# The last gather of two of a step's rows, fetched pixel by pixel from SyncE's and ScalarE's queues

## What is computed

```python
x = x + _L0_conv_ref(_gn(x), ...)   # 3x3 convolution
x = x + _L1_conv_ref(_gn(x), ...)   # deformable convolution, below
x = x + _L2_conv_ref(_gn(x), ...)   # focal modulation: depthwise 3x3, 5x5, 7x7 with gelu, gates
x = x + _L3_conv_ref(_gn(x), ...)   # layer norms, two gated products, a product over rows, a gate
```

```python
idx = (yi * W + xi).reshape(B, -1, 1)
v = jnp.take_along_axis(flat, idx, axis=1)
out = wa * gather(y0i, x0i) + wb * gather(y1i, x0i) + wc * gather(y0i, x1i) + wd * gather(y1i, x1i)
```

## Time and profile before

| | |
|---|---|
| median of 3 runs | 12372.07 us (12347.44 to 12374.3) |
| span of the profiled execution | 17350.5 us |
| gathers issued by GpSimd | 9216 |
| steps | 128 |
| granted TensorE clock, mean | 0.694 |
| HBM read, written | 1069 MB, 245 MB |

### The profile page before, as it was taken

One profiled execution on the slowest core, in us unless ns is written; L12 is line 12 of the kernel. 1 busy time (PEld: TensorE's weight loads), 2 busy tenths in 40 slices (PEclk: granted clock), 3 DMA queues, 4 the chain that ended last, 5 costly groups with the idle time before them and its releaser, 6 DMA issues.

```text
span 17350.5 us, 102336 instructions
## 1 busy us (share of the span) xinstructions
PE 8037.3 (46%) x30934; PEld 5581.5 (32%) x30934; DVE 5165.4 (30%) x5993; ACT 1769.5 (10%) x2822; POOL 8759.5 (50%) x9300
## 2 busy tenths in 40 slices
PE   4444444445345544443335555344325555443358
PEld 2223223223234432232224443232223443222245
DVE  2222222322333233233222233223223223222323
ACT  1001101110000011100000001110000001110014
POOL 4555555455554555455554455555555444545530
PEclk7667677667667776666667777666667777666679
DMA  2222222222223321222123321222112332122233
GB/s 78 68 60 66 78 62 70 72 61 77 61 75 98 98 60 48 63 80 59 43 61 99 98 84 45 57 77 68 46 52 77 98 98 61 48 64 77 60 124 118
DMA packets 878203, 1254.74 MB, mean 72 GB/s; under 512 B 183384, under 2 KB 663064, under 8 KB 859992
## 3 DMA queue, kind: packets, MB, share of 16 engines
q0 software_dynamic: 294912, 604.57, 13.7%
q1 hardware_dynamic: 511784, 596.71, 10.7%
q10 hardware_dynamic: 71344, 51.39, 0.9%
HBM read 1069.42 MB, written 245.43 MB: 76 GB/s over the span
## 4 chain that ended last, share of the span: by engine, by line
another core or an unknown queue 40%; PE 20%; issue 19%; DVE 10%; ACT 3%; PEldq 2%; PEld 1%; SPq 1%; DMA 1%; ACTq 1%; DVEq 1%
PE acc L1307 8%; PE stage L1163 6%; DVE srow L1685 5%; PE stage L1035 2%; PEldq L483 2%; DVE gathered L1678 2%; PE pt L1294 1%; ACT stt L1008 1%; PEld acc L1307 1%; PE stage L1102 1%; PE stage L1081 1%; DMA off<-offs 1%; DVE wtn L1647 0%; SPq L694 0%
## 5 line engine op out<-in xcount | busy, mean ns | idle before, releaser
L543 POOL DMA_INDIRECT gathered<-table,idx x9216 | 8708.9, 945 | 7844.0 <-issue 4412.7
L1307 PE MATMUL acc<-stt,room 128*128 128x256 f32 (+2 forms) x15360 | 4368.5, 438 | 4763.0 <-ACT stt L1008 2491.7
L1307 PEld LDWEIGHTS acc<-stt,room 128*128 128x128 f32 (+1 forms) x15360 | 3242.4, 221 | 5803.8 <-issue 2728.6
L1685 DVE TENSOR_REDUCE srow<-gathered 128x576 f32<-128x2304 f32 x512 | 2097.1, 4096 | 324.7 <-remote 207.2
L1163 PE MATMUL stage<-room 128*128 128x128 f32 x6784 | 1035.3, 303 | 1067.5 <-issue 1049.5
L1163 PEld LDWEIGHTS stage<-room 128*128 128x128 f32 x6784 | 962.5, 218 | 1139.8 <-issue 1134.0
L1678 DVE TENSOR_TENSOR gathered<-gathered,wtb 128x2304 f32<-128x2304 f32 x512 | 1304.4, 2548 | 1.2 <-issue 1.2
L1008 ACT ACTIVATE stt<-pt 128x1024 f32<-128x1024 f32 (+1 forms) x512 | 415.6, 812 | 8375.5 <-remote 4988.2
L1666 DVE SCALAR_TENSOR_TENSOR xs<-acc,fused,xr 128x256 f32<-128x256 f32 x128 | 61.7, 482 | 3747.9 <-PE acc L1307 2206.0
L1035 PE MATMUL stage<-room,mat 128*128 128x512 f32 (+1 forms) x1360 | 776.2, 694 | 841.1 <-issue 338.9
L1294 PE MATMUL pt<-mat,srow 128*128 128x128 f32 x2048 | 427.2, 337 | 1475.6 <-DVE srow L1685 1250.7
(11 more groups left out here) (212 smaller groups left out, 4575.2 us busy)
## 6 DMA issues: line engine op xcount, KB each, us to landing
gathered<-table,idx POOLq DMA_INDIRECT x9216
room<-toep SPq DMA_DIRECT2D x48, 1792.0 KB, 7.0
room<-toep SPq DMA_DIRECT2D x64, 1280.0 KB, 8.0
room<-toep SPq DMA_DIRECT2D x64, 768.0 KB
table<-room SPq DMA_DIRECT2D x64, 512.0 KB
toep<-in_taps SPq DMA_DIRECT2D x128, 224.0 KB
gathered<-toep SPq DMA_DIRECT2D x16, 1792.0 KB, 7.0
toep<-in_taps SPq DMA_DIRECT2D x128, 160.0 KB
```

The lines of the kernel that those rows point to most:

```text
L543: nc.gpsimd.indirect_dma_start(gat[r][:, k % K9 * G + k // K9, :], None, table[b].rearrange("(n e) -> n e", e=PAIR), bass.IndirectOffsetOn ...
L1307: ins = nc.tensor.matmul(sums_of[:, pairs, :], wk[0:kk, m, dx, at:at + P], stt[0:kk, slots, m, dx:dx + W], start=start and m == 0 and dx == 0,
L1685: nc.vector.tensor_reduce(srow[r % 2][:].rearrange("p (s c) -> p s c", c=CG), gat[r][:].rearrange("p s (q c) -> p s c q", q=4), AX.X, ALU. ...
```

## The change

Of two of a step's four rows, 3 and 0, the last of the 18 gathers is taken from GpSimd. For row 3 SyncE, for row 0 ScalarE fetches the same 128 entries with 128 DMAs of 512 bytes each.

- VectorE writes these 128 byte addresses (entry x 256 plus the group's offset) as integers into `pixel_at[r]` (two tensor_scalar of 128x1 a step), right after the indices.
- The engine turns the column into a row with one DMA (`pixel_row[r]`), waits for it and for the buffer's last sum, and then works in eight chunks: it reads 16 addresses into registers and issues 16 DMAs, one row of `gathered` each, from the table at that byte address.
- SyncE's chunks (`fetch`) stand at phases 0.5, 1, ... 4 of the same step. They are merged with SyncE's other instructions of the step; it waits for the sum of row 3 of the step before.
- ScalarE's chunks stand at 3r + 3 and 3r + 4, two after each row's copies, and serve row 0 of the next step; the first step's are fetched at the start, before the second tile of offsets.
- VectorE waits for 17 gathers and for the 128 pixels of such a row.
- To free semaphores, the four `lg_s` of the roots become one with a running count; that alters no order.

The diff, without the lines that only rename `lg_s`:

```diff
@@ -23,6 +23,7 @@
 U32 = mybir.dt.uint32
+U8 = mybir.dt.uint8
 ALU = mybir.AluOpType
...
@@ -46,6 +47,9 @@
 STEPS = NB * PER
+FETCHED = {3: GK - 1, 0: GK - 1}
+BY_SP, BY_ACT = 3, 0
+CHUNK = 16
 ENTRY = 4 * CG
...
@@ -120,6 +124,16 @@
         k = min((t, k) for k, t in enumerate(times) if t is not None)[1]
+        times[k] = next(flows[k], None)
+def merged(*flows):
+    times = [next(f, None) for f in flows]
+    while any(t is not None for t in times):
+        t, k = min((t, k) for k, t in enumerate(times) if t is not None)
+        yield t
         times[k] = next(flows[k], None)
...
@@ -255,6 +269,8 @@
         idx = sb("idx", [P, ROWS, GK], U32)
+        pixel_at = {r: sb(f"pixel_at{r}", [P, 1], I32) for r in FETCHED}
+        pixel_row = {r: sb(f"pixel_row{r}", [1, P], I32) for r in FETCHED}
         wtn = sb("wtn", [P, ROWS, GK, 4])
...
@@ -434,6 +450,13 @@
         turned_full, full_ready = sems("turned_full", "full_ready")
+        act_given, act_row_in = sems("act_given", "act_row_in")
+        pixels_given = {BY_SP: composed, BY_ACT: act_given}
+        pixel_row_in = {BY_SP: x_in[1], BY_ACT: act_row_in}
+        pixels_in = {BY_SP: x_in[2], BY_ACT: loaded}
+        GIVEN0 = {BY_SP: 2, BY_ACT: 0}
+        ROW0 = {BY_SP: 16, BY_ACT: 16}
+        PIXELS0 = {BY_SP: 16, BY_ACT: 16 * N_LOAD}
         (padded_c,) = sems("padded_c")
...
@@ -495,6 +518,21 @@
             return d[b].rearrange("c (h r) w -> r c h w", r=2)[par, :, ds(4 * t, 4), :]
+        def gathered_by_pool(r):
+            return GK - 1 if r in FETCHED else GK
+        def fetch_pixels(eng, engine, b, r, first):
+            k = FETCHED[r]
+            slot = k % K9 * G + k // K9
+            _, starts = nc.values_load_multi_w_load_instructions(
+                pixel_row[r][:, first:first + CHUNK], engines=[engine], min_val=0, max_val=4 * PAIR * (G * TABLE - 1),
+                skip_runtime_bounds_check_because="the coordinates are clipped to the image")
+            for p, start in enumerate(starts, first):
+                eng.dma_start(gat[r][p:p + 1, slot, :].bitcast(U8), table[b].bitcast(U8)[ds(start, 4 * ENTRY)].unsqueeze(0))\
+                    .then_inc(pixels_in[r], 16)
...
@@ -539,7 +577,7 @@
                         pool.sem_inc(started, 1)
-                        for k in range(GK):
+                        for k in range(gathered_by_pool(r)):
                             nc.gpsimd.indirect_dma_start(
...
@@ -760,7 +798,24 @@
+                def fetch(n, b, at):
+                    r = BY_SP
+                    yield at
+                    sp.wait_ge(pixels_given[r], GIVEN0[r] + n + 1)
+                    sp.dma_start(pixel_row[r][:], pixel_at[r][:]).then_inc(pixel_row_in[r], 16)
+                    sp.wait_ge(pixel_row_in[r], ROW0[r] + 16 * n + 16)
+                    sp.sem_inc(started, 1)
+                    sp.wait_ge(summed, ROWS * n + r + 1)
+                    sp.sem_inc(started, 1)
+                    for first in range(0, P, CHUNK):
+                        yield at + 4 * first / P
+                        fetch_pixels(sp, mybir.EngineType.SP, b, r, first)
                 def step(n, b, i):
+                    return merged(step_body(n, b, i), fetch(n, b, 0.5))
+                def step_body(n, b, i):
                     yield 0
...
@@ -998,8 +1053,31 @@
+                def give_row(n):
+                    act.wait_ge(pixels_given[BY_ACT], GIVEN0[BY_ACT] + n + 1)
+                    act.dma_start(pixel_row[BY_ACT][:], pixel_at[BY_ACT][:]).then_inc(pixel_row_in[BY_ACT], 16)
+                def row_given(n):
+                    act.wait_ge(pixel_row_in[BY_ACT], ROW0[BY_ACT] + 16 * n + 16)
+                    act.sem_inc(started, 1)
+                    act.wait_ge(summed, ROWS * n + BY_ACT + 1)
+                    act.sem_inc(started, 1)
+                def start():
+                    give_row(0)
+                    row_given(0)
+                    for first in range(0, P, CHUNK):
+                        fetch_pixels(act, mybir.EngineType.Activation, 0, BY_ACT, first)
                 def step(n, b, i):
+                    last = isinstance(n, int) and n == STEPS - 1
+                    nb = b + 1 if isinstance(i, int) and i == PER - 1 else b
+                    if not last:
+                        yield 1
+                        give_row(n + 1)
                     for r in range(ROWS):
...
@@ -1011,12 +1089,20 @@
                             .then_inc(st_ready, 1)
+                        if last:
+                            continue
+                        if r == 0:
+                            row_given(n + 1)
+                        for q in range(2 * r, 2 * r + 2):
+                            yield 3 * r + (3 if q % 2 == 0 else 4)
+                            fetch_pixels(act, mybir.EngineType.Activation, nb, BY_ACT, q * CHUNK)
...
                 act.sem_inc(right_entries, 2)
-                drive(act, meet, step, lambda: None, {"modulate": ln_and_exp, "close": ln_and_exp},
+                act.sem_inc(pixel_row_in[BY_ACT], 16)
+                drive(act, meet, step, start, {"modulate": ln_and_exp, "close": ln_and_exp},
                       {"conv_norm": norm, "shift": shift, "conv_shift": lower_part, "table_norm": norm,
...
@@ -1649,6 +1735,10 @@
                     then(tt(idxn[:], entry, gbase[:], ALU.add))
+                    for r, k in FETCHED.items():
+                        dve.wait_ge(pixel_row_in[r], ROW0[r] + 16 * n)
+                        ts(pixel_at[r][:], entry[:, r, k:k + 1], 4.0 * PAIR, 4.0 * PAIR * TABLE * (k // K9),
+                           ALU.mult, ALU.add).then_inc(pixels_given[r], 1)
                     then(ts(xy(base, 1), xy(base, 1), float(ROWS), None, ALU.add))
...
@@ -1669,7 +1759,9 @@
                     yield 3 * r
-                    dve.wait_ge(landed[r], 16 * GK * (n + 1))
+                    dve.wait_ge(landed[r], 16 * gathered_by_pool(r) * (n + 1))
+                    if r in FETCHED:
+                        dve.wait_ge(pixels_in[r], PIXELS0[r] + 16 * P * (n + 1))
                     if give:
...
```

More of the change, by code:

```diff
@@ L447, in build @@
                                              "sums", "dw_chain", "mixed"))
-        q_p, q_s, m_p, xo_s, m_cen_p, m_sq_s, m_var_p, m_lg_s, m_rs_s, m_y_s, m_o_p, m_added = sems(
-            "q_p", "q_s", "m_p", "xo_s", "m_cen_p", "m_sq_s", "m_var_p", "m_lg_s", "m_rs_s", "m_y_s",
+        q_p, q_s, m_p, xo_s, m_cen_p, m_sq_s, m_var_p, m_rs_s, m_y_s, m_o_p, m_added = sems(
+            "q_p", "q_s", "m_p", "xo_s", "m_cen_p", "m_sq_s", "m_var_p", "m_rs_s", "m_y_s",
             "m_o_p", "m_added")
         ca_in = sems(*(f"ca_in{u}" for u in range(4)))
-        t_cen_p, t_sq_s, t_var_p, t_lg_s, t_rs_s, t_y_s, ab_p, g_p, ab_s, g_s = sems(
-            "t_cen_p", "t_sq_s", "t_var_p", "t_lg_s", "t_rs_s", "t_y_s", "ab_p", "g_p", "ab_s", "g_s")
+        t_cen_p, t_sq_s, t_var_p, t_rs_s, t_y_s, ab_p, g_p, ab_s, g_s = sems(
+            "t_cen_p", "t_sq_s", "t_var_p", "t_rs_s", "t_y_s", "ab_p", "g_p", "ab_s", "g_s")
         abg_out = sems(*(f"abg_out{u}" for u in range(4)))
@@ L459, in build @@
         ab_in, s_out = (sems(*(f"{n}{u}" for u in range(4))) for n in ("ab_in", "s_out"))
-        c_cen_p, c_sq_s, c_var_p, c_lg_s, c_rs_s, c_y_s, c_o_p, lin_s, res_s = sems(
-            "c_cen_p", "c_sq_s", "c_var_p", "c_lg_s", "c_rs_s", "c_y_s", "c_o_p", "lin_s", "res_s")
+        c_cen_p, c_sq_s, c_var_p, c_rs_s, c_y_s, c_o_p, lin_s, res_s, lg_s = sems(
+            "c_cen_p", "c_sq_s", "c_var_p", "c_rs_s", "c_y_s", "c_o_p", "lin_s", "res_s", "lg_s")
         s_in, g_in, res_out = (sems(*(f"{n}{u}" for u in range(4))) for n in ("s_in", "g_in", "res_out"))
@@ L904, in depthwise, with roots @@
                         act.dma_start(group(mixd, b, 2 * i + u), mix[u]).then_inc(mix_out[u], 16)
-                def roots(n, count, eps_, var_p, lg_s, y_s, rs_s):
+                def roots(n, count, eps_, var_p, y_s, rs_s, before):
                     for u in range(count + 1):
@@ L912, in roots @@
                         if u:
-                            act.wait_ge(lg_s, n(u - 1) + 1)
+                            act.wait_ge(lg_s, n(u - 1) + before + 1)
                             act.wait_ge(y_s, n(u - 1) + 1)
@@ L933, in modulate @@
                     yield 5
-                    roots(n, flight(b), eps[:, 1:2], m_var_p, m_lg_s, m_y_s, m_rs_s)
+                    roots(n, flight(b), eps[:, 1:2], m_var_p, m_y_s, m_rs_s, 2 * b * TB)
                 def operands(b, i):
@@ L944, in operands @@
                     ln_and_exp(b)
-                    roots(n, flight(b), eps[:, 0:1], t_var_p, t_lg_s, t_y_s, t_rs_s)
+                    roots(n, flight(b), eps[:, 0:1], t_var_p, t_y_s, t_rs_s, (2 * b + 1) * TB)
                     yield 7
@@ L989, in close @@
                     yield 5
-                    roots(n, flight(b), eps[:, 0:1], c_var_p, c_lg_s, c_y_s, c_rs_s)
```

(1 more changed line is left out.)

## The result

The changed kernel takes 13453.6 us (median of 4 runs, 13447.5 to 13459.9), the kernel before, on the same chip, 12373.2. The ratio is 1.087, with a 95% interval of 1.086 to 1.089: 1080 us slower, and 650 above the upper end of the range.

A forecast was written before the change was run, and what follows sets the result against it. GpSimd's gather pitch was taken to bound the kernel before, and SyncE's fetch chain the changed depthwise steps: 12372 - 320 (gathers saved) + 390 (depthwise loss) = 12442, say 12440 us, range 12040 to 12800.

The forecast's parts named there:

- The bound and the gathers' saving: GpSimd's gather pitch of 1.248 us bounds every step; two gathers fewer in each of 128 steps save 320 us.
- The gaps come from being recorded: Profiled execution: some 5000 us of gaps between gathers come from an engine slowed by recording; unrecorded, GpSimd hardly waits.
- The price of the fetch: On SyncE and ScalarE: a step's 128 pixel DMAs and address reads occupy the engine for 54 us, bounds 45 to 92.
- hidden: Rival: the depthwise chain stays short enough that GpSimd remains the bound, 12052 to 12100 us; chance 0.27.
- SyncE's block in the depthwise stage: In all 24 depthwise steps the second bands queue behind SyncE's whole fetch; three images lose 390 us.
- T to T: Depthwise step from one end of row 3's sum (T) to the next: 110 us, 23 more than GpSimd's 87.4.
- 20 + 54 = 74 is under 87.4: ScalarE's 20 us of work a step plus 54 of fetch stays below GpSimd's 87.4 us for 70 gathers.
- In other stages I take nothing: Outside the depthwise stage SyncE's late loads leave room; close comes near 95 us in 4 steps, absorbed; loss nothing.
- 54 us are absorbed per image: Depthwise stage: GpSimd's lead of three rows absorbs 54 us of the chain's excess once per image.
- The start, "nothing, at worst 10 us once": Kernel start: ScalarE fetches 128 pixels before the second offsets tile; costs nothing, at worst 10 us once.
- The two queues: Rival: SyncE's and ScalarE's issues hinder each other, 0.13 us more for each that overlaps; 12850 us, chance 0.05.
- The full sequencer: Rival: register reads cost 0.29 us each, a fetch 83 us on its engine; some 14300 us, chance 0.09.

The follow-up runs named there:

- e3: The kernel before with 17 gathers in rows 3 and 0 and nothing fetched in their place: 12047.7 us, ratio 0.974.
- e4: The kernel before, unchanged, profiled once more: 12372.9 us, with a profiled span of 12371.1 us.
- e1: The changed kernel without ScalarE's fetch (only SyncE fetches, row 0 keeps 18 gathers): 12634.2 us, ratio 1.021.
- e5: e1 with SyncE's eight chunks in bands, three of them ahead of the depthwise stage's second bands: 12218.3 us, ratio 0.989.
- e2: The changed kernel without SyncE's fetch (only ScalarE fetches, row 3 keeps 18 gathers): 12435.9 us, ratio 1.005.
- e12: e2 without ScalarE's last two chunks of eight, so 32 of 128 pixels aren't fetched: 12216.6 us, ratio 0.987.
- e13: e2 without ScalarE's first two chunks of eight, so 32 of 128 pixels aren't fetched: 12220.6 us, ratio 0.988.
- e10: e2 with ScalarE's eight chunks in two runs of four, behind the copies of rows 0 and 1: 13717.0 us, ratio 1.110.
- e7: The changed kernel with SyncE's chunks in bands as in e5, ScalarE's chunks as they were: 13131.4 us, ratio 1.063.
- e14: e7 without ScalarE's last two chunks (32 pixels not fetched): 12227.5 us, ratio 0.988.
- e15: e7 without ScalarE's first two chunks (32 pixels not fetched): 12787.3 us, ratio 1.034.

## Why the prediction was wrong, point by point

**The bound and the gathers' saving: right.** e3 gives 323.6 us for the 320 of the earlier trace rows.

**The gaps come from being recorded: wrong.** e4 recorded has none. The sum from 12372 was still right to make, since the gaps do not belong to the usual run.

**The price of the fetch: right.** 54 us was taken, bounds 45 to 92. A block took 50.8 us from its first pixel's issue, and with the first read of 1.2 us it is 52. A pixel was 0.33 us with 0.36 taken, as its issue was 0.223 to 0.228 and not the 0.28 drawn from the earlier trace rows. A chunk's read was 1.2 us with 1 taken. What decided for "hidden" was 38 us, so that rival fell for SyncE's one block.

**SyncE's block in the depthwise stage: right in mechanism, and in size in part by luck.** 112.2 us from T to T were measured with 110 predicted. The block began at T + 14.1 and not T + 8.5, as the pixel row took 7.9 us from its issue (4044.41) to what waited for it (4052.32), with 2.3 taken for the landing; the block was 2 us shorter, and from its end to TensorE's first pass it was 6.3 us, with 8.4 taken. The 390 us were for 70 gathers a step; for e1's 71 (88.8 us) the same sum gives 3 x (8 x 21.2 - 54) = 347 us, and 424 were measured (e1 against its floor): the first depthwise step of each image took 126 to 129 us and the others 112 to 116. e5, which moves nothing but those chunks, gives all but 8 to 29 us of it back.

**ScalarE, "20 + 54 = 74 is under 87.4": the step that failed.** Occupancy was compared where the chain counted. The earlier trace rows gave the 20 us of work, but not that each chunk stands between two turns with VectorE, on which row 0's pixels, the roots and gelus and so the sums depend. ScalarE's fetch cost 226 us alone (e2), by a threshold between 39 and 52 us (e12, e13), and up to 1507 with the same pixels in two runs of four (e10 against 12210). A row of before could have told it: in the earlier trace rows VectorE's sum at 5741.28 follows on an activation of ScalarE at 5738.53, with ScalarE itself waiting 4.15 us for TensorE. ScalarE is idle there because it waits as a link of the chain, not because it has time to spare.

**"In other stages I take nothing": the larger miss.** The steps of the changed kernel less those of e3 give 1366 us, and its first sum comes 42 later: together 1408, where the runs have 1406. The depthwise steps are 24 x (116.9 - 90.1) = 643 of it. The others were put at nothing: close 12 x (106.2 - 87.9) = 220, operands 12 x (99.3 - 87.8) = 138, triangle 6 x (109.5 - 86.9) = 136, the first stages' tables 12 x (96.3 - 87.7) = 103, modulate 12 x (92.3 - 85.2) = 85, all other stages 190, while the steps between the images are 152 shorter than in e3. The first close steps, 139 to 141 us, are 155 of the close stage's 220, and the first depthwise steps, 142 to 152, are 152 of the 643: the change of stage, where a late engine holds all, was not in the sum either. For SyncE alone the claim held: e1 and e5 average 85.8 and 87.8 us in the close stage. ScalarE's pairs were what was missed, and through the sigmoids, their store and the offsets table they also delayed SyncE's own start.

**"54 us are absorbed per image": right for one fetch, too much for two.** GpSimd's lead can be read from the timelines, as the time from the start of row 3's last gather to the end of that row's sum. In the fifth depthwise step of e1:

```profile
3957.77 0.94 POOL L581 DMA_INDIRECT gathered<-table,idx  x1 [0.30 <-issue]
...
4044.50 4.10 DVE L1779 TENSOR_REDUCE srow<-gathered 128x576 f32<-128x2304 f32 x1
```

That is 90.8 us. In e1 it is 11 us in the step ahead of each depthwise stage, 48 to 51 in its first step, and from the third to the last 91 to 94; in the operands stage it is back at 10 to 12. The stage's 24 steps are 623 us longer than 71 gathers, 424 us were lost, so some 66 us an image were absorbed, with 54 predicted. In the changed kernel it is 44, 23 and 21 us ahead of the stage in the three images, 82 to 99 in it, mostly 91, and then 48 to 110 through modulate, operands, triangle and close; only the last steps of an image, behind the close stage, three of them of 61 to 84 us, bring it back to 10. So it does come back once an image, as the prediction had it, but not between the stages, and what the later stages hold up is lost with little left to absorb it: beyond its pitch GpSimd waits some 520 us in the depthwise steps, 244 in close, 183 in modulate, 111 in triangle, 88 in operands and some 200 in the first image's stages, of 1445.

**The start, "nothing, at worst 10 us once": too low.** The first row 3's sum ended at 319.4 us, in e3 at 277.1, some 42 us later. GpSimd's first wait for it came only behind gather 210, so it went out of the lead at first; how much of it stayed to the end is not known.

**The rivals.** The two queues don't hinder each other: the issue medians are 223 and 228 ns with both engines fetching as with one. The Trainium skill (Perfetto Trace Analysis, DMA Instruction, HWDGE) says that the descriptor generator is shared and locked; no row here shows a wait for it. The full sequencer fell with the read's 0.075 us an address (1.2 / 16). The Trainium skill (DMA: Bandwidth & Descriptors, Issuing engines are not separate DMA queues) holds that more issuing engines save only the issue time, usually small. Here 256 gathers fewer to issue are worth 323.6 us of the whole (e3), and with 128 of them replaced from SyncE's queue 133 us are left (e5: 12351.4 - 12218.3).

Why in e7 the first pair's removal is worth so much less over the whole run than the last's, when in the close stage they are nearly equal, the lead shows in part. The steps in the table differ mostly in the depthwise stage (6.1 us less against 1.7) and the operands (10.4 against 7.4). In e14 the depthwise steps of 93 us fit into the lead, which grows from 30 to 57 us in the first image's stage, and GpSimd waits 29 us in all three, as in e3 (31). In e15 the steps of 97 find the lead used up by the third step (74 to 78 us from there on), and it waits 181. What stays open is how much of e14's 180 us above e3 is SyncE's chain and how much the three pairs left. A kernel in which both rows are fetched whole and that beats e5 was not found.

## What to carry to other kernels

Before giving work to an engine that looks idle, find the chain through a step in which it is a link, and add the new work to that chain wherever it stands between two turns, with the steps at a change of stage looked at by themselves; its busy share does not show whether there is room (ScalarE was busy for 13 to 14% here). The loss is the chain's excess over the bound, so it starts suddenly (39 us free, 52 us for some 217) and two additions cost more than their sum. Cut queue blocks so that the load that is waited for passes between them: that alone turned a 2.1% loss (e1) into a 1.1% gain (e5).

## What was not expected of the hardware

A DMA of one 512-byte row at a register's address occupied its queue for 0.33 us with everything around it (0.22 to 0.23 us of issue, 0.03 of MOVE), on SyncE and ScalarE alike and at the same time. One instruction read 16 addresses from SBUF into registers in 1.2 us. The mean spacing of the gathers on GpSimd, waits left out, was 1.249 to 1.255 us in every kernel, while up to 256 other DMAs a step were issued beside them. And one profiled execution of before had a span of 17350 us (granted clock 0.694) where another had 12371 (0.77); what caused its 5000 us of gaps no run here shows.
